# A fused sequence model on one core: the time step added on TensorE, a fourth input product on GpSimd in odd iterations, dtu placed later, expert rows loaded at once

## The reference

```python
for i in range(NUM_LAYERS):
    x = mamba_block(layer_norm(x, ...), ...) + x
# in mamba_block
u = silu(conv(xs) + cb); dt, Bc, Cc = split(u @ Wx.T)
dt = softplus(dt @ Wdt.T + bdt)          # the time step
A = -exp(Alog)
h = exp(dt_t * A) * h + dt_t * B_t * u_t # one step of the scan
y = sum_over_states(h * C_t)
y = (y + u * Dp) * silu(z);  return y @ Wo.T
# dense experts
expert_outs = (silu(h @ Wg[e]) * (h @ Wu[e])) @ Wd[e]
# routed experts: each token's two rows are gathered, gelu(rows @ w_gate) @ w_down, weighted and added back
```

## Time and profile before

| | |
|---|---|
| median of 3 runs | 2603.98 us (2603.61 to 2604.18) |
| profiled execution, its own time | 2603.44 us |
| its span, first to last instruction | 2601.7 us |
| busy over the span: TensorE, VectorE, ScalarE, GpSimd | 89%, 79%, 60%, 79% |
| mean granted clock of TensorE | 0.974 of full |
| one iteration of the first half | 54.50 us |
| chain that ended last | GpSimd's additions to out (L1546) |

### The profile page before, as it was taken

The page is one execution under the profiler, slowest core; times in us unless marked ns, Lnnn a source line. Parts: engine busy times, 40 slices in busy tenths (PEclk is TensorE's granted clock), DMA queues, the critical chain, the costliest instruction groups (busy, mean ns, idle before and its releaser), DMA issues. The chain is left out here.

```text
span 2601.7 us, 22564 instructions
## 1 busy us (share of the span) xinstructions
PE 2318.5 (89%) x6064; PEld 1023.4 (39%) x6064; DVE 2055.6 (79%) x2028; ACT 1555.7 (60%) x2432; POOL 2045.6 (79%) x1269
## 2 busy tenths in 40 slices
PE   6588888888888999999999999999998899999594
PEld 4233333333333333343443333333333344444373
DVE  4799999999999999999999999999999343333221
ACT  3576777776777677777766767777765223222221
POOL 4599999999998899999999999999999332321366
PEclk9799999999999999999999999999999999999797
DMA  7466545654445766776667676766676400100353
GB/s 222 186 217 209 182 161 184 215 206 160 144 163 186 256 243 233 238 244 228 230 231 240 220 238 234 244 231 227 234 245 220 144 21 10 36 9 9 89 123 36
DMA packets 216929, 464.96 MB, mean 179 GB/s; under 512 B 29468, under 2 KB 109154, under 8 KB 216802
## 3 DMA queue, kind: packets, MB, share of 16 engines
q1 hardware_dynamic: 204818, 455.30, 51.3%
q0 software_dynamic: 11264, 7.98, 2.0%
q10 hardware_dynamic: 720, 0.23, 0.1%
HBM read 440.00 MB, written 23.99 MB: 178 GB/s over the span
## 5 line engine op out<-in xcount | busy, mean ns | idle before, releaser
L893 DVE TENSOR_TENSOR_SCAN hh<-decays,psdB 128x1024 f32<-128x1024 f32 x512 | 1165.7, 2283 | 58.9 <-ACT decays L715 18.6
L1030 POOL TENSOR_TENSOR products<-hh,Clo 128x1024 f32<-128x1024 f32 x408 | 961.4, 2360 | 112.1 <-DVE hh L893 111.1
L452 PE MATMUL psY<-products,ident 128*128 128x512 f32 x1708 | 831.9, 607 | 120.4 <-POOL products L1030 73.1
L715 ACT ACTIVATE decays<-dt,Acur 128x508 f32<-128x508 f32 x1024 | 667.4, 708 | 6.0 <-DVE hh L893 5.6
L452 PEld LDWEIGHTS psY<-products,ident 128*128 128x128 f32 x1708 | 311.5, 191 | 567.8 <-issue 350.4
L882 DVE TENSOR_TENSOR psdB<-psT,Blo 128x1024 f32<-128x1024 f32 x395 | 484.2, 1226 | 29.7 <-DMA Blo<-rows 1.8
L1458 DVE TENSOR_TENSOR ac<-sg,d_bank 128x512 f32<-128x512 f32 x135 | 92.8, 688 | 225.1 <-PE d_bank L1308 207.1
L432 PE MATMUL psW<-xnT,wcur 128*128 128x512 f32 x496 | 229.1, 604 | 41.8 <-DMA diag<-diags_l 22.9
L1030 POOL TENSOR_TENSOR products<-hh,late 128x1024 f32<-128x1024 f32 x104 | 244.0, 2366 | 18.3 <-PE psY L452 18.3
L1356 ACT ACTIVATE sg<-d_bank 128x512 f32<-128x512 f32 x135 | 80.6, 597 | 244.7 <-PE d_bank L1304 244.6
L1034 POOL TENSOR_TENSOR products<-products 128x512 f32<-128x512 f32 x170 | 215.7, 1269 | 13.3
(11 more groups left out here) (215 smaller groups left out, 2975.0 us busy)
## 6 DMA issues: line engine op xcount, KB each, us to landing
Blo<-rows SPq DMA_DIRECT2D x280, 512.0 KB, 5.7
Clo<-rows SPq DMA_DIRECT2D x280, 512.0 KB, 4.9
late<-rows SPq DMA_DIRECT2D x104, 512.0 KB, 6.1
wcur<-taps_l SPq DMA_DIRECT2D x31, 512.0 KB
fw<-in_Wg SPq DMA_DIRECT2D x36, 256.0 KB, 5.2
fw<-in_Wu SPq DMA_DIRECT2D x36, 256.0 KB, 4.5
fw<-in_Wd SPq DMA_DIRECT2D x36, 256.0 KB, 5.2
disp<-fw SPq DMA_DIRECT2D x16, 528.0 KB, 7.1
```

The source lines that it names most:

```text
L452: ins = pe.matmul(psY[:, :], lhsT=ident[:, :], rhs=gg[k % NGB][:, j, :], start=False, stop=(k % NK == NK - 1 and j == last - 1))
L715: ins = act.activation(dA[k % NDA][:, j, :, 1:T], dt[i % 2][:, c, :, 1:T], ACT.Exp, scale=Acur[i % 2][:, s:s + 1])
L893: dve.tensor_tensor_scan(out=hh[k % NHB][:, :, :].rearrange("p c t -> p (c t)"), data0=dA[k % NDA][:, :, :, :].rearrange("p c q t -> p (c ...
L1030: ins = pool.tensor_tensor(gg[k % NGB][:, :, :], hh[k % NHB][:, :, :], tile(Clo, Chi, slot(i, s)), ALU.mult)
```

## The change

1. *Time step.* For iterations t = 1 to 14, TensorE makes relu + logarithm: `add_step` at steps 10 and 11 (st0, st1), each two matmuls with the identity into psW; ScalarE copies each to `dt` at its step 14, behind added and ahead of decay(i, 14) (`place_step`). GpSimd's `time_step` stays for t = 15 and later. Whoever waited for `dt_ok` now waits for that copy (`stepped`).
2. *Fourth product.* Step 14 is given too, in odd iterations below 13; GpSimd makes it at its step 10, ScalarE copies it at its step 15.
3. *dtu.* GpSimd makes dtu at step 12, ahead of gate0 (`late_dtu`), and ScalarE places its first half at step 1 of the iteration itself instead of step 15 of the one before.
4. *Semaphores.* rs1 and rs2, exp_ok and ln_ok become one each; `weighted` is replaced by `homed`.
5. *Seam.* At the end of the dense phase TensorE gets 32 matmuls whose result nobody reads.
6. *Expert phase.* `dx` has 8 buffers; SP issues the row loads of all experts first, without waiting, and then the weight loads; the loads are awaited in four batches (expert 0, 1, 2 and 3, 4 to 7).

```diff
-ACT_AT = {1: ["params", "dtu1", "norm"], ... 14: ["added"], 15: ["centre", "dtu0"]}
-GIVEN = {4: 0, 9: 5, 13: 8}
-POOL_AT = {1: ["gate1"], 6: ["rstd"], 10: ["dt"], 11: ["dtu"], 12: ["gate0"]}
+PE_AT = {... 9: ["out"], 10: ["st0"], 11: ["st1"], 12: ["T"], 14: ["x0"]}
+ACT_AT = {1: ["dtu0", "params", "dtu1", "norm"], ... 14: ["added", "st0", "st1"], 15: ["centre"]}
+GIVEN = {4: 0, 9: 5, 13: 8, 14: 10}
+POOL_AT = {1: ["gate1"], 6: ["rstd"], 10: ["dt"], 11: ["dtu"], 12: ["late_dtu", "gate0"]}
...
+def summed(what, t):
+    return what not in ("st0", "st1") or 1 <= t < FIRST
...
         def assisted(i, k):
-            return i < RING0 and k in GIVEN
+            return i < RING0 and k in GIVEN and (k != 14 or i % 2 == 1)
...
+        def stepped(eng, t):
+            if 1 <= t < FIRST:
+                eng.wait_ge(wfree, W["st1", t] + 1)
+            else:
+                eng.wait_ge(dt_ok, 1 if t == 0 else t - FIRST + 2)
...
                 def load_x(d):
-                    sp.wait_ge(dt_ok, FIRST + NF * d)
+                    stepped(sp, FIRST + NF * d - 1)
...
+                def add_step(t, c):
+                    pe.wait_ge(soft_ok, 2 * t)
+                    pe.wait_ge(wfree, W[f"st{c}", t])
+                    pe.matmul(psW[:, :], lhsT=ident[:, :], rhs=dt[t % 2][:, c, :, :].rearrange("p q t -> p (q t)"), start=True, stop=False)
+                    pe.matmul(psW[:, :], lhsT=ident[:, :], rhs=soft[:, c, :], start=False, stop=True).then_inc(wready, 1)
...
+                def place_step(t, c):
+                    act.wait_ge(wready, W[f"st{c}", t] + 1)
+                    act.activation(dt[t % 2][:, c, :, :].rearrange("p q t -> p (q t)"), psW[:, :], ACT.Copy).then_inc(wfree, 1)
...
                 def decay(i, k):
-                        act.wait_ge(dt_ok, i + 1)
+                        stepped(act, i)
...
+                            if what in ("st0", "st1") and 1 <= i + 1 < FIRST:
+                                place_step(i + 1, int(what[-1] == "1"))
...
-                            if what == "dtu0" and i + 1 < RING0:
-                                place_dtu(i + 1, 0)
+                            if what == "dtu0" and 0 < i < RING0:
+                                place_dtu(i, 0)
...
                 def time_input(t):
-                    pool.wait_ge(dt_ok, t + 1)
+                    stepped(pool, t)
+                    at_least(pool, gave, helped(NSTEP * t))
...
-                            if what == "dt" and i + 1 < NIT:
+                            if what == "dt" and FIRST <= i + 1 < NIT:
                                 time_step(i + 1)
-                            if what == "dtu" and i + 1 < NIT:
+                            if what == ("late_dtu" if i + 1 < FIRST else "dtu") and i + 1 < NIT:
                                 time_input(i + 1)
...
                 pe.matmul(psN, lhsT=ones[:, :], rhs=cnt[:, G, 0, :], start=True, stop=True).then_inc(counted, 1)
+                pe.wait_ge(silued, CR + NST * NDT)
+                for r in range(32):
+                    pe.matmul(psG[r % 2][:, :], lhsT=ident[:, :], rhs=wgu[:, 0, 0, :], start=True, stop=True)
...
-        NDX, NEO = 3, 3
-        dx = [[sb(f"dx{c}_{p}", [128, NCH, RW]) for p in range(NDX)] for c in range(2)]
+        NEO = 3
+        BATCH = [0, 1, 2, 2, 3, 3, 3, 3]
+        dx = [[sb(f"dx{c}_{p}", [128, NCH, RW]) for p in range(NE)] for c in range(2)]
...
                 def load_rows(e):
-                    at_least(sp, evac, CR + NHT * (e - 2))
...
-                for e in range(NE + 1):
-                    if e < NE:
-                        load_rows(e)
-                    if e > 2:
-                        load_weights(e - 1)
+                for e in range(NE):
+                    load_rows(e)
+                for e in range(2, NE):
+                    load_weights(e)
...
-                        dve.wait_ge(x_ld[p], 32 * (e // NDX + 1))
+                        dve.wait_ge(x_ld[BATCH[e]], 32 * BATCH.count(BATCH[e]))
```

More of the change, by code:

```diff
@@ L40 @@
 PRE = ("x0", "x1", "z0", "z1", "bcdt", "dt0", "dt1")
-AHEAD = {"x0": 2, "x1": 1, "z0": 1, "z1": 1, "bcdt": 1, "dt0": 1, "dt1": 1, "outT": -1, "out": -1, "T": 2}
-PE_AT = {0: ["x1"], 1: ["z0"], 2: ["z1"], 4: ["bcdt"], 6: ["dt0"], 7: ["dt1"], 8: ["outT"], 9: ["out"], 12: ["T"], 14: ["x0"]}
+AHEAD = {"x0": 2, "x1": 1, "z0": 1, "z1": 1, "bcdt": 1, "dt0": 1, "dt1": 1, "st0": 1, "st1": 1, "outT": -1, "out": -1, "T": 2}
+PE_AT = {0: ["x1"], 1: ["z0"], 2: ["z1"], 4: ["bcdt"], 6: ["dt0"], 7: ["dt1"], 8: ["outT"], 9: ["out"], 10: ["st0"], 11: ["st1"], 12: ["T"], 14: ["x0"]}
 SUM_FIRST = (15,)
-ACT_AT = {1: ["params", "dtu1", "norm"], 2: ["turn0"], 4: ["sums1", "x0"], 5: ["x1"], 6: ["z0"], 7: ["z1", "silu"], 8: ["bcdt"], 10: ["turn1"], 11: ["dt0"],
-          12: ["dt1", "sums0", "softplus"], 13: ["outT"], 14: ["added"], 15: ["centre", "dtu0"]}
-GIVEN = {4: 0, 9: 5, 13: 8}
-POOL_AT = {1: ["gate1"], 6: ["rstd"], 10: ["dt"], 11: ["dtu"], 12: ["gate0"]}
+ACT_AT = {1: ["dtu0", "params", "dtu1", "norm"], 2: ["turn0"], 4: ["sums1", "x0"], 5: ["x1"], 6: ["z0"], 7: ["z1", "silu"], 8: ["bcdt"], 10: ["turn1"], 11: ["dt0"],
+          12: ["dt1", "sums0", "softplus"], 13: ["outT"], 14: ["added", "st0", "st1"], 15: ["centre"]}
+GIVEN = {4: 0, 9: 5, 13: 8, 14: 10}
+POOL_AT = {1: ["gate1"], 6: ["rstd"], 10: ["dt"], 11: ["dtu"], 12: ["late_dtu", "gate0"]}
 G_AT = [-11, -9, -7, -6, -5, -4, -2, 0, 1]
@@ L79, in psw_uses @@
                 t = i + AHEAD[what]
-                if 0 <= t < NIT:
+                if 0 <= t < NIT and summed(what, t):
                     order.append((what, t))
@@ L188, in wave_phase @@
         first_use = {"x0": dB[0][:, 0, :], "x1": dB[0][:, 1, :], "bcdt": dB[0][:, 0, :], "dt0": dB[0][:, 1, :]}
-        names = ("wcur_ld wready wfree dbu da scan prod half red stat moments rs1 rs2 rstd_ok centred skipped par_ok kept_ok exp_ok ln_ok dt_ok dtu_ok placed silu_ok "
+        names = ("wcur_ld wready wfree dbu da scan prod half red stat moments rs rstd_ok centred skipped par_ok kept_ok soft_ok dt_ok dtu_ok placed silu_ok "
                  "ycopied ygated gave moved cleared zero zeroed x_ld x1_ok x_st gated gfree sg_ok scaled upped acted downed sum_ok").split()
-        (wcur_ld, wready, wfree, dbu, da, scan, prod, half, red, stat, moments, rs1, rs2, rstd_ok, centred, skipped, par_ok, kept_ok, exp_ok, ln_ok, dt_ok, dtu_ok, placed, silu_ok,
+        (wcur_ld, wready, wfree, dbu, da, scan, prod, half, red, stat, moments, rs, rstd_ok, centred, skipped, par_ok, kept_ok, soft_ok, dt_ok, dtu_ok, placed, silu_ok,
          ycopied, ygated, gave, moved, cleared, zero, zeroed, x_ld, x1_ok, x_st, gated, gfree, sg_ok, scaled, upped, acted, downed, sum_ok) = (sem(n) for n in names)
@@ L504, in work @@
                         t = i + AHEAD[what]
-                        if not 0 <= t < NIT:
+                        if not 0 <= t < NIT or not summed(what, t):
                             continue
+                        if what in ("st0", "st1"):
+                            add_step(t, int(what[-1] == "1"))
                         if what in PRE:
@@ L661, in pre @@
                         act.wait_ge(wready, W[what, t] + 1)
-                        at_least(act, dt_ok, t)
+                        if t > 0:
+                            stepped(act, t - 1)
                         if c == 0 and t >= FIRST and (t - FIRST) % NF == 0:
@@ L1490, in sparse_phase @@
         psT, psH, psE = bank[0:2], bank[2:6], bank[6:8]
-        x_ld, x_first = [sem(f"x_ld{p}") for p in range(NDX)], sem("x_first")
-        picked, homed, weighted, trans, copied, upped, gelud, downed, evac, added = (
-            sem(n) for n in "picked homed weighted trans copied upped gelud downed evac added".split())
+        x_ld, x_first = [sem(f"x_ld{b}") for b in range(4)], sem("x_first")
+        picked, homed, trans, copied, upped, gelud, downed, evac, added = (
+            sem(n) for n in "picked homed trans copied upped gelud downed evac added".split())
         tokens = out.rearrange("b t d -> (b t) d")
```

33 lines of the change are left out of this document (16 added, 17 removed).

## The result

| | before | after |
|---|---|---|
| median, same chip | 2604.08 us (2603.61 to 2604.47, 4 runs) | 2655.47 us (2650.25 to 2656.09, 4 runs) |
| ratio | | 1.0193, 95% interval 1.018 to 1.0205 |
| profiled execution, own time / span | 2603.44 / 2601.7 us | 2650.25 / 2648.5 us |
| iterations 1 to 12, in all | 654.26 us | 692.63 us |
| last TensorE work ahead of the seam (the matmul into psN) | 2418.77 | 2454.69 |

Iterations are counted here from scan 0 to the next scan 0 on VectorE.

The account below looks back on a forecast made before the run. VectorE and GpSimd were level as busiest, the 54.50 us period set by VectorE's scans and a ScalarE-TensorE chain. First half 27.8 plus tail 7.6, 35.4 us on 2603.44, forecast 2639 us; range 2612 to 2662, own range 2628 to 2650.

Parts of the forecast that it names:

- Scan 14 waits for the copies: Iteration end: decay 14 queues behind st1's copy on ScalarE; 2.6 us stall, scan 15 3.5 late in odd iterations.
- What comes back: Before scan 7: x0 starts sooner behind scan 15, returning 0.81 us in each iteration that follows a lengthened one.
- the length of an iteration on a TensorE at full clock: First half, iterations 1 to 12: even ones 1.8 us longer, odd ones 2.7, in all 27.8.
- The meeting at the seam: Between dense and expert phase: engines wait for TensorE's warm-up, so expert 0's loads go out 12.9 us later.
- Rival (b): Seam: TensorE doesn't hold it up, only its first transposes wait; tail 2.9 us, total 2634; chance 0.10.
- rival (c): Seam: the warm-up matmuls run cold throughout, 24 us more, total 2663; chance 0.09.
- The clock after the warm-up: Expert phase start: TensorE still warm after a 4.6 us gap; first transposes and up product 2.85 us faster.
- rival (e): Behind the warm-up: the clock falls in the 4.6 us gap, total 2642; chance 0.15.
- Rows at once: Expert phase: row loads leaving together shorten the 5.64 us wait of GpSimd's additions; 2.5 us gained.
- (a): First half: copies come in time, 17.5 us off, tail +7.6, total 2594; chance 0.08.
- (d): First half: half of scan 14's stall is absorbed, 27.8 becomes 14, total 2625; chance 0.10.
- (f): Whole kernel: gains and losses meet within 0.2%, first half with half of (a)'s gain; chance 0.05.

Follow-up runs that it names:

- Kernel 6: After with ScalarE's two copies of the time step moved behind decays 14 and 15: 2652.6 us, ratio 1.018.
- kernel 7: After with the time step's copies behind decays 14 and 15 and GpSimd's time input (dtu) behind its product 13: 2617.97 us, ratio 1.0051.
- Kernel 4: After without the fourth product, so VectorE makes step 14's input term in all iterations: 2649.72 us, ratio 1.0172.
- Kernel 10: After with copies behind decays 14 and 15, time input behind product 13, no fourth product, no seam matmuls (rows at once kept): 2599.26 us, ratio 0.9979.
- Kernel 2: Before with only the 32 matmuls at the end of the dense phase added: 2618.01 us, ratio 1.0048.
- kernel 3: Before with only the expert rows of all eight experts loaded at once: 2603.13 us, ratio 0.9994.
- Kernel 5: Before with only the fourth input product on GpSimd in odd iterations, the time step staying GpSimd's addition: 2619.11 us, ratio 1.0068.
- kernel 11: Kernel 10 with the fourth product kept, its copy ahead of the first copy of the time step: 2605.27 us, ratio 1.0006.
- kernel 12: Kernel 10 with five 512-column matmuls on TensorE behind the seam: 2596.96 us, ratio 0.9971.

## Why the prediction was right, and where it was not

The forecast of 2639 had the sign and four of its mechanisms right. The median is 2655.47: inside the range (2612 to 2662), 5 us above the forecast's own range, and 16 above the number. That it is inside owes something to luck: the upper end stood for a warm-up that runs cold, and the largest part of what came on top, the dips of the clock, had no term.

- *Scan 14 waits for the copies.* Right in place, cause and size: 2.70 for 2.6 in even iterations. In odd ones I had scan 15 3.5 late; 4.80 less the 1.30 that is saved is 3.5. The proof by experiment is kernels 6 and 7: with the copies behind the decays the wait ahead of scan 14 goes, and with dtu moved too the iterations are about as long as in before. Kernel 6 adds what the prediction did not have: this cure alone fails, because the copies' other customer, GpSimd's dtu, is then late and holds up TensorE's x0, and dips follow there.
- *What comes back* was put at 0.8 an iteration. The wait ahead of scan 7 fell from 1.38 to 0.77, so 0.6. Even iterations are 2.00 longer for 1.8, odd ones 2.98 for 2.7: six of each are 29.9, for 27.8 in the sum.
- *The term that was mis-sized* is the length of an iteration on a TensorE at full clock. The prediction took every instruction of the first half at its duration in before. In after the clock dips in some iterations, and iterations 1 to 12 are 38.4 longer, 8.5 more than the 29.9. Of the 8.5, 7.3 are waits ahead of scan 14 in the five iterations with a dip 33 us in; 0.35 in iteration 5 and 0.8 at the end of iteration 12 come without one. Kernel 4 shows 1.30 per dip, iteration by iteration. What a dip costs depends on what stands in it. ScalarE waits for the sums there in after, so a slow matmul is passed on in full; where nobody waits at that place, the dip is free. Kernel 10 has six dips between 200 and 850 us and no iteration from 2 to 11 over 54.33. Kernel 2, with before's first half, has four between 600 and 800 us, 33 us into their iterations, which take 54.5 as in the earlier trace rows. Near the start of an iteration, on the way to x0, a dip costs without those waits too: 2.2 in iteration 1 of kernel 2, some 1.7 in kernel 6.
- *The meeting at the seam.* Right: ScalarE goes on when TensorE's queue lets it, the loads go out 12.7 later for 12.9. The 12.7 is the 48.6 between the loads less the 35.9 that the dense phase ends later. Rival (b) is refuted by the 32.70 put down to PEq, rival (c) by the 30.27 us that the matmuls took.
- *The clock after the warm-up.* Wrong, and rival (e) right: 2.85 was counted as gained and nothing was; the first product even took 0.6 more. The step that failed was reading the end of the kernel (the us from 2571) as the time that the clock stays up: there it fell some 5 us after the last matmul, here it was at 0.50 in the window from 2488, 2.7 us after it. That an idle gap between bursts loses the clock is what the Trainium skill says ("TensorE: Matmul & The Clock Gate", Part 1); the trace agrees, 0.50 in the window ahead of the transposes.
- *Rows at once.* The wait of 5.64 did fall to 3.56, and the delay shrank from 13.5 at the second expert's additions to 10.9 at the end, 2.6 for the forecast's 2.5. By itself (kernel 3) the edit gains too little to be told from nothing. The Trainium skill, "DMA: Bandwidth & Descriptors" (Arbitration), would have had expert 0's additions share with the rows in flight. The trace does not show it: expert 0's first and fifth addition are 7.72 us apart (2504.88, 2512.60) with some 300 GB/s in flight, as in before (2455.82, 2463.54) with under 45. But that is GpSimd's pace of issuing; the wait ahead of expert 1's additions, where a late landing would show, grew only from 3.92 to 4.27, and is put down to VectorE.
- *Rivals (a), (d), (f)* needed a shorter wait at scan 14, and it was longer.

For the profiled execution: 29.9 + 8.5 in iterations 1 to 12, of which iteration 0 and the second half return 2.5, and 10.9 behind it, 46.8, where the prediction had 27.8 + 7.6 = 35.4. Two of its smaller sums are off without weight: the 2.85 is 2.79 from its own terms, and the lower end of its range is the stall at a quarter of its price, not a third.

Why the dips come is open. Each of the ten in after begins in or within 2 us behind an idle gap of TensorE (0.99 or 2.67 us), and the one shown of kernel 6 behind one of 3.53; but the gap of 1 us stands in every iteration, in before too, and mostly no dip follows. Kernel 5 has them without a time step on TensorE and kernel 2 with before's own first half, so they do not belong to the added sums. The other runs of after are up to 6 us longer than the profiled one. They have no trace, but their mean granted clock is 0.968 or 0.969 for 0.972, which fits more dips.

## What to carry to other kernels

A copy that waits for another engine should stand behind the work on its own queue that does not need it; where the queue is written by hand, look at every consumer of that copy, because moving it back only shifts the wait to the next one (3.7 and -1.1 us alone, hardly more than the spread, 38.0 together). Giving an engine's work away pays only where that engine is the one waited for: VectorE's 1.30 was lost three times, in after (kernel 4 is better without it) and in kernels 5 and 11. Work meant to warm TensorE up cost 11 to 13 us ahead of the last meeting of all engines and warmed nothing. Behind it and up to the first use (kernel 12) it did warm the first product, for 0.7 us, which the medians do not confirm.

## What the runs showed of the hardware

TensorE's clock can fall to 1.2 GHz for some 3 us in a stretch in which it is about 90% busy, at different places in executions of the same first half: none between 100 and 850 us in the trace of before, four between 600 and 800 us in kernel 2. In after each such fall begins in or within 2 us behind an idle gap of 1.0 or 2.7 us, but most such gaps are followed by none. What it costs depends on the place: 1.30 to 1.70 us at the sums that ScalarE waits for in after, some 2 us on the way to x0 (iteration 1 of kernel 2), nothing at the end of an iteration of after or 33 us into one of kernel 2.
